# One attention layer, unrolled over the batch: maxima alone in the double PSUM banks, three single banks for everything that ScalarE empties

## The chip, the core and the metric

The kernel runs on one core of a Trainium2 chip. A core has five engines that run their own instruction streams and wait for each other by semaphores: TensorE (PE in the profile, with PEld for its weight loads), VectorE (DVE), ScalarE (ACT), GpSimd (POOL) and SyncE (SP, which here only issues transfers). TensorE writes to PSUM alone, a memory of eight banks of 2 KB per partition; VectorE and ScalarE read it. The metric is the time of the program in microseconds (us) of device time.

## The reference

A pre-norm transformer layer for x of shape [8, 1024, 256]:

- attention: LayerNorm; q, k, v = three 256x256 products (q and v with a bias); the last 256 of 1024 positions of q and k are rotated (cos, sin, in bf16); 16 heads of 16; softmax(q k^T / 4) v in float32; a 256x256 product with bias; added to x.
- mixture of experts: LayerNorm; gate logits (16 experts), softmax; each expert takes its 128 best tokens of a batch entry, runs a gated 256-512-256 network, and adds the result, weighted, to those tokens; a shared expert of the same shape runs on all tokens.

The change touches attention alone.

## The kernel before, in words

Attention handles one batch entry of 1024 tokens in a **turn** (`turn`, eight of them). Turn 0 and turn 7 stand in the code by themselves; turns 1 to 6 are one loop body (`Fori` in `turns`). Sixteen heads make four groups `g` of four heads; four heads lie at partitions 0, 32, 64 and 96, so four products with 32 rows each can run in the array side by side (`tile_position`).

A turn has 64 **steps**. A step takes one group, one half of the queries (512) and one tile of 128 keys. TensorE computes four blocks of transposed scores (`score_bank`, L858, keys on the partitions, 512 queries in a bank), ScalarE turns each into exp(score/4) in SBUF (L714, tile `PR`), and TensorE multiplies these with the values into one accumulator bank (`weigh_values`, L872, `pv`). Eight steps fill the accumulator for a query half; ScalarE copies it out (`evacuate`, L678, tile `OT`).

The softmax needs each query's maximum before the exponential. So the same scores are computed a second time in the other orientation (L800, queries on the partitions, two heads by 512 keys in a double bank), and VectorE reduces them (L554, tile `MX`), one group ahead. GpSimd splits the maximum in three bf16 parts (`split_maxima`), TensorE transposes them (L807), VectorE copies them to SBUF and four small transfers write them into spare rows of the transposed queries `QT`, where a -1 in `KT` subtracts them from the scores.

All other work is a list of **items** that `slot_items` puts among the steps: `xt` (transposed normalised input), `qk` and `v` (the projections; each product is made of three float32r products, L61 to L63), `qkT` (transposed q and k, L792), `ot` (transposed weighted values, L813), `aot` and `proj` (output projection), `x2t` and `lg` (gate logits, L842), and `sc` and `nm` (maxima scores and their parts).

The eight banks: two double banks `ring`, through which every item goes in turn; three single banks `st` for the transposed scores; one for `pv`. Within a step TensorE issues three `score_bank`, the first half of the step's items, the fourth `score_bank`, the value product of the step before, and then the other items. An item waits until the item two before it has been emptied, mostly by VectorE (`consume`); ScalarE empties only a few. At the end of turns 0 to 6 both `v` items are computed with nothing beside them (`flush`).

The lines that the prediction touches:

```python
                        for j in range(3):
                            score_bank(b, g, s, j)
                        for item in items[:cut]:
                            fill(item, t, b)
                        score_bank(b, g, s, 3)
                        if g or s:
                            finish_step(t, b, g * STEPS + s - 1)
```

Of the kernel before, what the change touches and what calls it, by code (L numbers as in the profile page):

```python
# [65 lines left out]
def attention(nc, d, ident, SC, B):  # L66
# [3 lines left out]

# [5 lines left out]
    NQ = T // 512  # L76
    STEPS = NQ * TT
    ROPE_TILES = 2
    SC_TILES = 4 * TT
    HALF = SC_TILES // NQ  # L80
    LEAD = 8
    ST_BANKS = 3
    P_STEPS = 2

    def scores(grp, a, z):

        return [("sc", grp, n % HALF // (TT // NQ), n // HALF * (TT // NQ) + n % (TT // NQ)) for n in range(a, z)]

    def last_score(grp, qh):
        return ("sc", grp, 3, TT // NQ * (qh + 1) - 1)

    def slot_items(g, prev, more):


        t = g + 1
        base = (scores(g, HALF + LEAD, SC_TILES) + scores(t, 0, 2) + [("nm", g, 1)] + scores(t, 2, HALF + 4)
                + [("nm", t, 0)] + scores(t, HALF + 4, HALF + LEAD))
        steps = [[] for _ in range(STEPS)]
        for n, item in enumerate(base):
            steps[n * STEPS // len(base)].append(item)
        extra = {3: [("ot", g - 1, 1)], 11: [("ot", g, 0)]}
        extras = [{2: [("qkT", 2)], 4: [("aot", 0, 1)], 5: [("aot", 1, 1)], 7: [("proj", 0)], 12: [("proj", 1)]},
                  {1: [("qkT", 3)], 2: [("xt", 0, 1)], 4: [("xt", 1, 1)], 9: [("qk", 0, 1)], 12: [("qk", 1, 1)], 14: [("qk", 2, 1)]},  # L110
                  {1: [("qk", 3, 1)], 6: [("x2t", 0)], 8: [("qkT", G)], 13: [("x2t", 1)]},
                  {1: [("qkT", G + 1)], 5: [("lg", 0)], 6: [("lg", 1)]}][g]
        for s, items in extras.items():
            extra[s] = extra.get(s, []) + items
        for s, items in extra.items():
            steps[s] = items + steps[s]

        def kept(i):
            if not more and (i[0] in ("xt", "qk") or (i[0] in ("sc", "nm", "qkT") and i[1] >= G)):
                return False  # L120
            return prev or not (i[0] in ("aot", "proj", "x2t", "lg") or i[:2] == ("ot", -1))
        return [[i for i in st if kept(i)] for st in steps]

    PRO = ([("xt", 0, 0), ("xt", 1, 0)] + [("qk", n, 0) for n in (3, 0, 1, 2)] + [("qkT", 0), ("qkT", 1), ("v", 0), ("v", 1)]
           + scores(0, 0, HALF + 4) + [("nm", 0, 0)] + scores(0, HALF + 4, HALF + LEAD))
    TAIL = [("ot", -1, 1), ("aot", 0, 0), ("aot", 1, 0), ("proj", 0), ("proj", 1), ("x2t", 0), ("x2t", 1), ("lg", 0), ("lg", 1)]

    def split_late(item):


        return item[0] in ("xt", "aot") and item[2] == 1

    def by_scalar(item):
        return split_late(item) or item[0] == "x2t"

    KINDS = {"all": lambda item: True, "vector": lambda item: not by_scalar(item), "scalar": by_scalar,
             "split": split_late}

    class Turn:

        def __init__(self, b, prev=False, more=False):
            self.kind = b if isinstance(b, str) else "turn"
            self.slots = [slot_items(g, prev, more) for g in range(G)] if self.kind == "turn" else []
            self.flush = [("v", 0), ("v", 1)] if more else []
            self.order = {"prologue": PRO, "tail": TAIL,
                          "turn": [i for sl in self.slots for st in sl for i in st] + self.flush}[self.kind]
            self.b, self.prev = b, prev

        def total(self, kind="all"):
            return len([i for i in self.order if KINDS[kind](i)])

        def before(self, kind="all"):
            if self.kind == "prologue":
                return 0
            n = Turn("prologue").total(kind)
            if self.kind == "tail":
                return n + Turn(0, False, True).total(kind) + (B - 2) * Turn(1, True, True).total(kind) + \
                    Turn(1, True, False).total(kind)  # L160
            if not self.prev:
                return n
            return n + Turn(0, False, True).total(kind) + (self.b - 1) * Turn(1, True, True).total(kind)

        def upto(self, item, kind="all"):

            return self.before(kind) + len([i for i in self.order[:self.order.index(item) + 1] if KINDS[kind](i)])

        def pair(self, item):

            first = self if self.kind != "turn" or not self.prev else Turn(1, True, True)
            return (first.before() + self.order.index(item)) % 2

        def vector_done(self, item):

            assert not by_scalar(item)
            return self.upto(item, "vector")

    assert Turn(1, True, True).total() % 2 == 0 and B > 1

    def turns(engine, body):

        body(0, False, True)
        if B > 2:
            with engine.Fori(1, B - 1) as b:
                body(b, True, True)
        body(B - 1, True, False)

    ctx = ExitStack()
    with ctx:  # L190
# [10 lines left out]
        b_q = sb("b_q", [P, H], F32)  # L201
        b_v = sb("b_v", [P, H], F32)
        b_o = sb("b_o", [P, H], F32)
        cs_in = sb("cs_in", [P, 2, ROPE_TILES, HD], F32)
# [4 lines left out]
        XN = sb("XN", [P, TT, H], F32)  # L209
# [6 lines left out]
        QP = sb("QP", [P, TT, NH, QUAD], BF16)  # L216
        KP = sb("KP", [P, TT, NH, QUAD], BF16)
        KT = [sb(f"KT{g}", [P, T], BF16) for g in range(G)]
        QT = [sb(f"QT{g}", [P, T], BF16) for g in range(G)]
        VA = sb("VA", [P, TT, NH, QUAD], F32)  # L220
        PR = [sb(f"PR{n}", [P, 4, 512], F32) for n in range(P_STEPS)]
        OT = sb("OT", [P, 512], F32)
        AO = sb("AO", [P, TT, H], F32)
        W_raw = AO[:].rearrange("p a c -> p (a c)").rearrange("p (k n) -> p k n", k=KH)
        NS = sb("NS", [12, T], BF16)
        MX = sb("MX", [P, 2, 2, 4, TT], F32)
        NM = sb("NM", [P, TT, 4, 3], BF16)
        nmr = sb("nmr", [P, 4, TT], F32)
        RD = sb("RD", [P, 2, 4, 4], F32)
        stats = sb("stats", [P, TT, 6], F32)  # L230

# [10 lines left out]
        act_scratch = sb("act_scratch", [P, 2], F32)  # L242
        dve_scratch = sb("dve_scratch", [P, 1], F32)
        pool_scratch = sb("pool_scratch", [P, 2], F32)

        ring = [ctx.enter_context(nc.psum_tensor(f"ring{i}", [P, 2, 512], F32)) for i in range(2)]
        st_bank = [ctx.enter_context(nc.psum_tensor(f"st{i}", [P, 512], F32)) for i in range(ST_BANKS)]
# [8 lines left out]
        xn2_ready = [sem(f"xn2_ready{h}") for h in range(2)]  # L256
# [3 lines left out]
        high_ready = sem("high_ready")  # L260
        split_ready = sem("split_ready")
        powers_ready = sem("powers_ready")
        const_ready = sem("const_ready")
        fills = sem("fills")
        bias_added = sem("bias_added")
        xn_ready = [sem(f"xn_ready{h}") for h in range(2)]
        rstd_ready = [sem(f"rstd_ready{n}") for n in range(2)]
        ring_full = sem("ring_full")
        vector_freed = sem("vector_freed")
        scalar_freed = sem("scalar_freed")  # L270
        rope_done = sem("rope_done")
        maxima_ready = sem("maxima_ready")
        nm_ready = sem("nm_ready")
        nm_in = sem("nm_in")
        st_full = sem("st_full")
        st_free = sem("st_free")
        pv_done = sem("pv_done")
        ot_ready = sem("ot_ready")
        dve_own = sem("dve_own")
        pool_own = sem("pool_own")  # L280

        N_CONST = 6
# [4 lines left out]
        def _(sp):  # L287
# [7 lines left out]
            sp.dma_start(b_q[:], d["bq"].partition_broadcast(P)).then_inc(const_in, 16)  # L295
            sp.dma_start(b_v[:], d["bv"].partition_broadcast(P)).then_inc(const_in, 16)
# [5 lines left out]
            def load_maxima(grp, qh, after):  # L302

                sp.wait_ge(vector_freed, after)
                c = slice(512 * qh, 512 * qh + 512)
                for j in range(4):
                    sp.dma_start(QT[grp % G][QUAD * j + HD:QUAD * j + HD + 3, c],
                                 NS[3 * j:3 * j + 3, c]).then_inc(nm_in, 16)

            pro = Turn("prologue")  # L310
            load_maxima(0, 0, pro.vector_done(("nm", 0, 0)))

            def store_x1(b):
                sp.dma_start(rows("out", b), XR[:]).then_inc(x1_out, 16)

            def store_xn2(b):
                for h in range(2):
                    sp.wait_ge(xn2_ready[h], b + 1)
                sp.dma_start(rows("xn2", b), XN2[:]).then_inc(xn2_out, 16)

            def turn(b, prev, more):
                t = Turn(b, prev, more)
                if more:
                    for h in range(2):
                        sp.wait_ge(xn_ready[h], b + 1)
                    sp.dma_start(XA[:], rows("x", b + 1)).then_inc(xa_in, 16)
# [1136 lines left out]
```

## Time and profile before

| what | us |
|---|---|
| time, median of 3 runs | 2822.38 (2801.42 to 2823.64) |
| the profiled execution's own time | 2783.07 |
| its span, first to last instruction | 2781.2 |
| attention, first to last value product | 75.7 to 1850.8 |
| experts | from about 1885 |

The profile has, for each instruction, its engine, its line in the code, its start and its duration. A timeline row merges neighbours of the same kind; the bracket at its end says how long the engine sat idle before it and which instruction released it. TensorE's clock has two levels, 1.2 and 2.4 GHz; the granted clock of a stretch is given as a share of the higher.

### The profile page before, as it was taken

The page shows a single profiled execution, that of the slowest core. Times are in us where ns is not written, and L with a number is a line of the kernel's source. Part 1 is how long each engine was busy: PE and PEld are TensorE (multiplying, and loading weights), DVE is VectorE, ACT ScalarE, POOL GpSimd, SP SyncE. Part 2 cuts the span into 40 slices and gives each one's busy share as a digit, 9 for nine tenths or more (in the row PEclk, how much of TensorE's full clock was granted, in tenths as well). Part 3 has the DMA queues.
Part 4 walks back from the last instruction along what each step waited for, and adds up shares of the span by engine and source line. Part 5 has one row for each costly group of instructions (what it writes and reads, how often), then busy time and mean ns, then how long its engine had stood idle before and what let it go on. Part 6 is the DMA issues. An engine that isn't in the chain of part 4 may idle for free. (4 is left out here: it accounts for less than half of the span.)

```text
span 2781.2 us, 47867 instructions
## 1 busy us (share of the span) xinstructions
PE 2437.5 (88%) x16011; PEld 1353.1 (49%) x16011; DVE 1985.0 (71%) x2856; ACT 1466.4 (53%) x2656; POOL 779.2 (28%) x1242
## 2 busy tenths in 40 slices
PE   5888888888888888888888888878999799999997
PEld 3232332333333333233333232237888688888886
DVE  7888888688788788778878879725666455555553
ACT  0667667567566566656756767733233233333331
POOL 1121231132122132122213211100000266666664
PEclk8799999899999989899989999958999899999998
DMA  1000000010000000001000000103222244444443
GB/s 38 16 17 16 17 32 2 18 33 16 18 17 32 18 17 32 5 30 32 2 18 17 32 2 17 32 27 117 90 90 83 84 101 106 104 105 104 105 106 40
DMA packets 105805, 124.20 MB, mean 45 GB/s; under 512 B 8049, under 2 KB 92785, under 8 KB 105585
## 3 DMA queue, kind: packets, MB, share of 16 engines
q1 hardware_dynamic: 81008, 87.81, 9.9%
q0 software_dynamic: 24576, 33.57, 7.1%
q8 instruction: 124, 2.03, 0.3%
q14 instruction: 97, 0.79, 0.1%
HBM read 78.63 MB, written 41.94 MB: 43 GB/s over the span
## 5 line engine op out<-in xcount | busy, mean ns | idle before, releaser
L714 ACT ACTIVATE sb_PR<-st 128x512 f32<-128x512 f32 x2048 | 1092.0, 602 | 679.8 <-PE st L858 674.0
L554 DVE TENSOR_REDUCE sb_MX<-ring 128x2 f32<-128x1024 f32 x1024 | 1211.3, 1219 | 140.5 <-PE ring L800 111.6
L872 PE MATMUL pv<-sb_PR,sb_VA 128*32 128x512 f32 x4096 | 589.2, 650 | 1.2
L858 PE MATMUL st<-sb_QT,sb_KT 32*128 32x512 bf16 x2048 | 502.9, 405 | 81.7 <-ACT sb_PR L714 69.4
L800 PE MATMUL ring<-sb_KT,sb_QT 32*128 32x512 bf16 x2048 | 422.8, 406 | 151.0 <-DVE sb_MX L554 139.6
L359 POOL TENSOR_TENSOR sb_pool_scratch<-identity 128x1 f32<-128x1 f32 x284 | 55.2, 194 | 1346.1 <-DVE sb_MX L586 1327.4
L800 PEld LDWEIGHTS ring<-sb_KT,sb_QT 32*128 32x128 bf16 x2048 | 98.3, 92 | 679.9 <-DVE sb_MX L554 445.3
L1235 DVE TENSOR_TENSOR ex_HF<-ex_GL,ex_gu 128x512 f32<-128x512 f32 x128 | 87.5, 684 | 251.7 <-ACT ex_GL L1168 238.9
L1168 ACT ACTIVATE ex_GL<-ex_gu 128x512 f32<-128x512 f32 x128 | 76.5, 598 | 348.2 <-PE ex_gu L63 243.1
L858 PEld LDWEIGHTS st<-sb_QT,sb_KT 32*128 32x128 bf16 x2048 | 130.4, 92 | 225.1 <-ACT sb_PR L714 184.2
L1132 POOL DMA_INDIRECT out<-ex_YS,ex_rows_out x128 | 209.0, 1633 | 44.1 <-issue 43.6
L61 PE MATMUL ex_gu<-ex_XH,weights_high 128*128 128x512 f32 x512 | 200.8, 392 | 2.4 <-DVE ex_XL L1227 2.4
L62 PE MATMUL ex_gu<-ex_XL,weights_high 128*128 128x512 f32 x512 | 200.5, 392 | 0.0
L63 PE MATMUL ex_gu<-ex_XH,weights_low 128*128 128x512 f32 x512 | 200.2, 391 | 0.0
L1089 POOL TENSOR_TENSOR ex_pool_scratch<-identity 128x1 f32<-128x1 f32 x96 | 35.2, 366 | 526.7 <-POOLq L932 380.7
L872 PEld LDWEIGHTS pv<-sb_PR,sb_VA 128*32 128x32 f32 x4096 | 82.8, 111 | 160.0 <-issue 92.2
L61 PE MATMUL ex_y<-weights_high,ex_HH 128*128 128x256 f32 x512 | 148.1, 289 | 2.9 <-DVE ex_HL L1239 2.9
L62 PE MATMUL ex_y<-weights_low,ex_HH 128*128 128x256 f32 x512 | 145.5, 284 | 0.0
L63 PE MATMUL ex_y<-weights_high,ex_HL 128*128 128x256 f32 x512 | 145.5, 284 | 0.0
L1110 POOL DMA_INDIRECT ex_XG<-xn,ex_rows_in x128 | 126.1, 985 | 40.2 <-issue 39.6
L1168 ACT ACTIVATE sh_GL<-sh_gu 128x512 f32<-128x512 f32 x64 | 38.2, 597 | 177.0 <-PE sh_gu L63 177.0
L1235 DVE TENSOR_TENSOR sh_HF<-sh_GL,sh_gu 128x512 f32<-128x512 f32 x64 | 43.7, 683 | 104.4 <-ACT sh_GL L1168 104.2
(160 smaller groups left out, 3946.7 us busy)
## 6 DMA issues: line engine op xcount, KB each, us to landing
sb_XA<-x SPq DMA_DIRECT2D x8, 1024.0 KB, 5.6
sb_XR<-x SPq DMA_DIRECT2D x8, 1024.0 KB, 5.3
out<-sb_XR SPq DMA_DIRECT2D x8, 1024.0 KB, 4.5
xn<-sb_XN SPq DMA_DIRECT2D x8, 1024.0 KB, 4.5
sh_XG<-xn SPq DMA_DIRECT2D x16, 512.0 KB, 5.6
sh_X<-out SPq DMA_DIRECT2D x16, 512.0 KB, 5.0
weights<-WgT SPq DMA_DIRECT2D x16, 512.0 KB, 4.2
weights<-WuT SPq DMA_DIRECT2D x16, 512.0 KB, 6.2
```

The source lines that it names most:

```text
L61: nc.tensor.matmul(out, a_hi, b_hi, start=first, stop=False)
L62: nc.tensor.matmul(out, a_hi, b_lo, start=False, stop=False)
L63: return nc.tensor.matmul(out, a_lo, b_hi, start=False, stop=last)
L554: out = nc.vector.reduce_max(MX[:, grp % 2, half, 2 * pair:2 * pair + 2, qt], R[:], AX.X)
L714: nc.scalar.activation(PR[step % P_STEPS][:, j, :], st_bank[n % ST_BANKS][:], ACT.Exp, scale=0.25).then_inc(st_free, 1)
L800: out = nc.tensor.matmul(R[:, n, :], QT[grp % G][r, P * qt:P * qt + P], KT[grp % G][r, 512 * half:512 * half + 512], start=True, stop=True ...
L858: nc.tensor.matmul(st_bank[n % ST_BANKS][:], KT[g][r, P * kt:P * kt + P], QT[g][r, 512 * qh:512 * qh + 512], start=True, stop=True, tile_p ...
L872: out = nc.tensor.matmul(pv_bank[QUAD * j:QUAD * j + QUAD, :], VA[:, kt, 4 * g + j, :], PR[step % P_STEPS][:, j, :], start=(kt == 0), stop ...
L1110: nc.gpsimd.indirect_dma_start(out=XG[k % 2][:, t, :], out_offset=None, in_=d["xn2"], in_offset=bass.IndirectOffsetOnAxis(ap=rows_in[:, b: ...
L1132: nc.gpsimd.indirect_dma_start(out=d["out"], out_offset=bass.IndirectOffsetOnAxis(ap=rows_out[:, b:b + 1], axis=0), in_=YS[k % 2][:, t, :] ...
L1168: nc.scalar.activation(GL[f % 2][:], gu[f % 2][:, 0, 0:N], ACT.Gelu).then_inc(gelu_ready, 1)
L1235: nc.vector.tensor_tensor(HF[f % 2][:], GL[f % 2][:], gu[f % 2][:, 1, 0:N], ALU.mult).then_inc(hf_ready, 1)
```

## The change

Attention is written anew; the experts are as before.

- No loop: all 8 x 64 = 512 steps `V` stand in the code one after the other.
- The double banks `ring` hold only scores for maxima (`score_rows`, two per step, 12 steps ahead, `LEAD`). VectorE does these reductions, and its statistics, but no longer empties other items.
- The three single banks are now called `rot`. The transposed scores (`score_turned`) and every other item pass through them in one order (`ORDER`), and ScalarE empties all of them (`empty`). Items are cut to the size of one bank, so there are more, smaller ones; at most one stands in a step (`BESIDE`).
- Within a step TensorE issues maxima scores, transposed scores 0 and 1, maxima scores, transposed scores 2 and 3, then the item, then the value product of two steps before (`LAG`).
- The maxima's parts are written by GpSimd into spare columns of `QP`, and q is transposed once more for each half group (item `q2`); the small transfers are gone.
- The bias of q is added on TensorE by two products with one row; that of v is folded into the output bias once. `v` items stand in steps 49 to 58 and `VA` and `QP` exist twice. The projection's result goes by ScalarE to `PJ`, and GpSimd adds it to the residual.

```diff
-    ST_BANKS = 3
-    P_STEPS = 2
+    LEAD, LAG = 12, 2
+    ROT = 3
+    P_STEPS = 3
+    BESIDE = {
+        0: ("aot", -1, 0, 0), 1: ("aot", -1, 1, 0), 2: ("qT", 0, 2, 0), 3: ("ot", 7), 4: ("qT", 0, 2, 1),
+        5: ("proj", -1, 0), 6: ("q2", 1), 7: ("aot", -1, 0, 1), 8: ("aot", -1, 1, 1), 9: ("proj", -1, 1),
+        11: ("ot", 0), 12: ("proj", -1, 2), 14: ("q2", 2), 15: ("proj", -1, 3), 16: ("qT", 0, 3, 0), 17: ("qT", 0, 3, 1),
+        19: ("ot", 1), 20: ("xt", 1, 0, 0), 21: ("xt", 1, 1, 0), 22: ("q2", 3), 23: ("xt", 1, 0, 1), 24: ("xt", 1, 1, 1),
+        26: ("qk", 1, 6), 27: ("ot", 2), 28: ("qk", 1, 7), 30: ("q2", 4), 31: ("qk", 1, 0), 33: ("qk", 1, 1),
...
-        body(0, False, True)
-        if B > 2:
-            with engine.Fori(1, B - 1) as b:
-                body(b, True, True)
-        body(B - 1, True, False)
...
+            def bank(item):
+
+                n = PLACE[item]
+                if n >= ROT:
+                    pe.wait_ge(rot_done, n - ROT + 1)
+                return rot[n % ROT]
...
+            for V in range(-LEAD, LAST):
+                m = 2 * (V + LEAD)
+                if m < CHECKS:
+                    score_rows(m)
+                if V >= 0:
+                    for j in range(2):
+                        score_turned(V, j)
+                if m < CHECKS:
+                    score_rows(m + 1)
+                if V >= 0:
+                    for j in range(2, 4):
+                        score_turned(V, j)
+                for item in beside(V):
+                    fill(item)
+                if V >= LAG:
+                    weigh_values(V - LAG)
...
+            for V in range(-LEAD, LAST):
+                if V >= 0:
+                    for j in range(4):
+                        empty(("ex", V, j))
+                        if j == 2 and V >= 9 and V % 8 == 1:
+                            evacuate((V - 9) // 8)
+                for item in beside(V):
+                    empty(item)
```

How it moves instructions on TensorE, at a step with an `ot` item in turn 0. Before (`ring` L800 is for maxima, `st` L858 the transposed scores, L813 the item, L872 the values):

```order
L872 MATMUL pv<-sb_PR,sb_VA 32x512 x4
L800 MATMUL ring<-sb_KT,sb_QT 128x512 x2
L858 MATMUL st<-sb_QT,sb_KT 128x512 x3
L813 MATMUL ring<-identity,sb_OT 128x128 x4
L800 MATMUL ring<-sb_KT,sb_QT 128x512 x2
L858 MATMUL st<-sb_QT,sb_KT 128x512
L872 MATMUL pv<-sb_PR,sb_VA 32x512 x4
```

Now (L773 is for maxima, `rot` L786 the transposed scores, L740 the item, L797 the values):

```order
L797 MATMUL pv<-sb_PR,sb_VA 32x512 x4
L773 MATMUL ring<-sb_KT,sb_QT 128x512 x2
L786 MATMUL rot<-sb_QT,sb_KT 128x512 x2
L773 MATMUL ring<-sb_KT,sb_QT 128x512 x2
L786 MATMUL rot<-sb_QT,sb_KT 128x512 x2
L740 MATMUL rot<-identity,sb_OT 128x128 x4
L797 MATMUL pv<-sb_PR,sb_VA 32x512 x4
```

The item has moved from ahead of the fourth transposed score to behind it, and from a double bank to the rotation of three.

On ScalarE, around the copy of the accumulator. Before, in turn 0, it stood between the first and the second exponential of a step (in the loop body, where each instruction has a row):

```order
L714 ACTIVATE sb_PR<-st 128x512
L720 ISA
L678 COPY sb_OT<-pv 128x512
L713 REGISTER_ALU
L714 ACTIVATE sb_PR<-st 128x512
```

Now it stands between the third and the fourth, and the other items (L600, L604 and L605, L623) follow the fourth:

```order
L591 ACTIVATE sb_PR<-rot 128x512 x4
L600 COPY sb_XT<-rot 128x512
L591 ACTIVATE sb_PR<-rot 128x512 x3
L641 COPY sb_OT<-pv 128x512
L591 ACTIVATE sb_PR<-rot 128x512 x5
L604 CAST sb_QP<-rot 128x16x16
L605 CAST sb_KP<-rot 128x16x16
```

The copy waits for the value product that the same step issues last.

## Rows read from the trace of the kernel before

**Rows 1.** The page: TensorE's granted clock in 40 equal slices, in tenths.
```profile
PEclk8799999899999989899989999958999899999998
```

**Rows 2.** Groups by line: count, busy us, mean ns, idle us before them, releaser.
```profile
L714 ACT ACTIVATE sb_PR<-st 128x512 f32<-128x512 f32 x2048 | 1092.0, 602 | 679.8 <-PE st L858 674.0
L554 DVE TENSOR_REDUCE sb_MX<-ring 128x2 f32<-128x1024 f32 x1024 | 1211.3, 1219 | 140.5 <-PE ring L800 111.6
L678 ACT COPY sb_OT<-pv 128x512 f32<-128x512 f32 x64 | 37.1, 580 | 2.5 <-PE pv L872 2.5
L414 POOL TENSOR_TENSOR sb_AL<-sb_XT,sb_AH 128x1024 fp32r<-128x1024 f32 x14 | 33.1, 2364 | 1.1
```

**Rows 3.** Windows: length, PE, PEld, DVE, ACT, POOL busy us, clock, DMA share, GB/s.
```profile
494.00:1640.00 1146.00, 984.47 (x6950) 376.99 (x6946) 928.56 (x1292) 725.28 (x1359) 277.99 (x545) 0.93 0.06 20
```

**Rows 4.** Timeline (start, length, engine, line): first scores of turns 0, 1, 7.
```profile
71.19 0.61 PE L858 MATMUL st<-sb_QT,sb_KT 32*128 32x512 bf16 x3 [0.44 <-DMA sb_QT<-sb_NS]
...
282.39 0.39 PE L858 MATMUL st<-sb_QT,sb_KT 32*128 32x512 bf16 x3
...
1638.10 0.39 PE L858 MATMUL st<-sb_QT,sb_KT 32*128 32x512 bf16 x3
```

**Rows 5.** Timeline, a step without other items, turn 0.
```profile
118.12 0.45 PE L858 MATMUL st<-sb_QT,sb_KT 32*128 32x512 bf16 x3
118.67 2.06 ACT L714 ACTIVATE sb_PR<-st 128x512 f32<-128x512 f32 x4 [0.60 <-PE st L858]
119.32 0.38 PE L858 MATMUL st<-sb_QT,sb_KT 32*128 32x512 bf16 x1 [0.44 <-ACT sb_PR L714]
119.63 1.07 PE L872 MATMUL pv<-sb_PR,sb_VA 128*32 128x512 f32 x8
```

**Rows 6.** Timeline, another such step, turn 7.
```profile
1789.84 1.07 PE L872 MATMUL pv<-sb_PR,sb_VA 128*32 128x512 f32 x8
1790.84 0.86 PE L858 MATMUL st<-sb_QT,sb_KT 32*128 32x512 bf16 x3
1792.32 1.07 PE L872 MATMUL pv<-sb_PR,sb_VA 128*32 128x512 f32 x8
```

**Rows 7.** Timeline, a step with an `ot` item, turn 1.
```profile
681.10 1.07 PE L872 MATMUL pv<-sb_PR,sb_VA 128*32 128x512 f32 x8
...
682.82 0.66 PE L813 MATMUL ring<-identity,sb_OT 128*128 128x128 f32 x4
...
684.49 1.06 PE L872 MATMUL pv<-sb_PR,sb_VA 128*32 128x512 f32 x8
```

**Rows 8.** Timeline, TensorE at the end of turn 1: `v` items, loop, next turn.
```profile
495.39 0.39 PE L61 MATMUL ring<-sb_WH,sb_XH 128*128 128x256 f32 x1
...
501.13 0.28 PE L63 MATMUL ring<-sb_WH,sb_XL 128*128 128x256 f32 x1
503.18 0.61 PE L858 MATMUL st<-sb_QT,sb_KT 32*128 32x512 bf16 x3 [1.77 <-issue]
...
508.18 0.60 PE L800 MATMUL ring<-sb_KT,sb_QT 32*128 32x512 bf16 x2 [3.55 <-DVE sb_MX L554]
```

**Rows 9.** Timeline, other items on TensorE: `qk`, `qkT`, `lg`.
```profile
608.61 0.50 PE L61 MATMUL ring<-sb_WH,sb_XH 128*128 128x512 f32 x1
...
611.24 0.39 PE L63 MATMUL ring<-sb_WH,sb_XL 128*128 128x512 f32 x1
...
569.86 0.62 PE L792 MATMUL ring<-sb_identb,sb_QP 128*128 128x128 bf16 x8
...
688.98 1.96 PE L842 MATMUL ring<-sb_gw,sb_XT 128*128 128x16 f32 x16
```

**Rows 10.** Timeline, turn 7 when no maxima are left: value products, low clock.
```profile
1840.72 1.94 PE L872 MATMUL pv<-sb_PR,sb_VA 128*32 128x512 f32 x8
...
1844.48 1.94 PE L872 MATMUL pv<-sb_PR,sb_VA 128*32 128x512 f32 x8
```

**Rows 11.** Timeline, ScalarE ahead of TensorE, turn 1.
```profile
703.20 3.69 ACT L714 ACTIVATE sb_PR<-st 128x512 f32<-128x512 f32 x7
```

More of the change, by code:

```diff
@@ L75, in attention @@
     KH = H // P
-    NQ = T // 512
-    STEPS = NQ * TT
+    STEPS = G * 2 * TT
+    UNITS = 2 * G
+    LEAD, LAG = 12, 2
     ROPE_TILES = 2
-    SC_TILES = 4 * TT
-    HALF = SC_TILES // NQ
-    LEAD = 8
-    ST_BANKS = 3
-    P_STEPS = 2
[L92 to L177, printed above, removed]
@@ new lines, in attention @@
+    HEAD = ([("xt", 0, h, half) for half in range(2) for h in range(KH)] + [("qk", 0, i) for i in (6, 7, 0, 1, 2, 3, 4, 5)]
+            + [("qT", 0, 0, 0), ("qT", 0, 0, 1), ("bo",)])
+    TAIL = ([("ot", UNITS * B - 1)] + [("aot", B - 1, h, half) for half in range(2) for h in range(KH)]
+            + [("proj", B - 1, i) for i in range(4)] + [("x2t", B - 1, h, half) for half in range(2) for h in range(KH)]
+            + [("lg", B - 1, half) for half in range(2)])
+    ORDER = HEAD + [item for V in range(-LEAD, LAST)
+                    for item in ([("ex", V, j) for j in range(4)] if V >= 0 else []) + beside(V)] + TAIL
@@ L189, in attention, with done, check @@
+    PLACE = {item: n for n, item in enumerate(ORDER)}
+    assert len(PLACE) == len(ORDER)
+    def done(item):
+        return PLACE[item] + 1
+    def check(m):
+        unit, n = m // 16, m % 16
+        c = (2, 0, 3, 1)[n % 4]
+        return unit, c // 2, c % 2, 4 * (unit % 2) + n // 4
     ctx = ExitStack()
@@ L497, in normalise @@
-            def normalise(n, out, src, ready, own):
-                for k in range(RSQRT_STEPS):
-                    own.inc(rstd_step(n, k, own))
-                own.wait(dve)
+                step = rsqrt_step(nc, k, rstd[n][:], nt1[:], nt2[:], mv[n][:, :, 1])
+                if k == RSQRT_STEPS - 1:
+                    step.then_inc(rstd_ready[n], 1)
+                else:
+                    own.inc(step)
+            def normalise(n, b, out, src, ready):
+                dve.wait_ge(rstd_ready[n], b)
@@ L648, in _ @@
-            turns(dve, turn)
-            own = Tally(dve_own, HEAD + PER_FIRST + (B - 2) * PER + PER - LN_INCS)
-            tail = Turn("tail")
-            for item in TAIL[:3]:
-                consume(item, tail, B, own)
-            for half in range(2):
-                consume(("proj", half), tail, B, own)
-                x1_stands(tail.vector_done(("proj", half)), own)
-                statistics(1, XR, range(TT // 2 * half, TT // 2 * (half + 1)), own)
-            own.wait(dve)
-            dve.wait_ge(xn2_out, 16 * (B - 1))
@@ L742, in _ @@
[L742 removed]
+                empty(item)
+            gate_powers(B - 1)
         @block.tensor
@@ L902, in _ @@
+            for V in range(LAST - LAG, LAST):
+                weigh_values(V)
             for item in TAIL:
-                fill(item, Turn("tail"), B)
+                fill(item)
 KD, KF = D // P, F // P
```

896 lines of the change are left out of this document (434 added, 462 removed), and 5 rows, old and new, of the table BESIDE.

## The prediction

> **What bounds the kernel now.** I read the page first, then the groups by line, then the timeline of TensorE and ScalarE step by step. The groups show two engines with large reductions: ScalarE's exponentials are busy 1092 us and wait 674 us for the transposed scores; VectorE's maxima are busy 1211 us and wait little [rows 2]. In the middle turns VectorE is busy 929 of 1146 us, TensorE 984, ScalarE 725 [rows 3]. No engine is full, so the time is set by a chain that goes round between engines, and the question is how long it is in a step.
>
> A step with nothing beside it shows the chain. Three transposed scores start at 118.12; ScalarE starts at 118.67; the fourth score needs the bank of the first and starts at 119.32, which is 1.20 after the first; the values start at 119.63, 0.31 later [rows 5]. From the value product to the next step's scores it is 1.00 [rows 6]. Together 1.00 + 1.20 + 0.31 = 2.51 us; rows 6 show 2.48 from one value product to the next. Four exponentials take 2.06 in a row [rows 5], two maxima about 2.4 [rows 2]: both fit under it. **The bound is this loop through three single banks**, to which items add.
>
> A turn takes (1638.10 - 282.39) / 6 = 226.0 us in the middle, turn 0 takes 211.2 [rows 4], turn 7 takes 213 (the attention's end is in the table).
>
> **What goes.** At the end of turn 1 TensorE computes `v` alone (495.39 to 501.3), sits 1.77 us with nothing to wait for, and then 3.55 us for VectorE [rows 8]. All of it goes. The Trainium skill (Runtime: NRT & Kernel Launch, "Instruction fetch mechanics") says that a taken branch breaks the sequential prefetch; the 1.77 us agree, and by that rule alone the change should gain. Also VectorE's waits for items, and TensorE's for VectorE, go; I count them in by building the new turn from steps rather than by subtracting. The transfers of the maxima go too; they are hidden behind a lead of several steps before, and their successor `q2` stands two steps ahead of its use and three behind the last maximum, some 9 us for five GpSimd operations on 16 elements: nothing for that.
>
> **What comes: the item now lies on the chain.** Before, the first half of a step's items stood in the 1.20 us in which TensorE waits for the first exponential anyway. An `ot` item made a step of 3.39 us [rows 7], part of it a wait for VectorE. Now the item comes behind the fourth score and takes the bank after it in the rotation, so it waits for the second exponential: four take 2.06 [rows 5], so one comes every 0.52 us. The item starts 0.52 behind the fourth score, and then its own length f, and then the values. So a step with an item takes 1.00 + 1.20 + 0.52 + f = 2.72 + f; one without, 2.5.
>
> The lengths f at the high clock:
> - four float32 transposes: 0.66 with the drain of the last [rows 7], about 0.50 to the next instruction; 12 (`xt`, `aot`, `x2t`) and 8 `ot`: 10.0 us
> - eight bf16 transposes 0.62 with the drain [rows 9], about 0.45; 8 `qT` 3.6, and 8 `q2` of four at 0.3 2.4
> - `qk`: eleven intervals in 2.63 us [rows 9], six products and their lead 1.5, two short bias products 0.25 (estimate, from the 0.12 below): 8 x 1.75 = 14.0
> - `v` and `proj`: 47 intervals in 5.74 us, 0.122 each [rows 8]; twelve products 1.5; 8 x 1.5 = 12.0
> - `lg`: 1.96 [rows 9], 1.9 to the next; 2 x 1.9 = 3.8
>
> Sum 45.8. `BESIDE` has 54 items: 10 x 2.5 + 54 x 2.72 + 45.8 = 217.7 us.
>
> **The accumulator's copy.** Once in eight steps ScalarE copies `pv` between the third and fourth exponential, and waits for the value product that TensorE issues last in that step, behind the item. Counted from the fourth score: item from 0.52 to 1.02, values to 2.09 (their length is 1.07 [rows 5]), copy from about 2.2, fourth exponential 2.7, item's copy 3.2, next exponential 3.7. Without the copy the next exponential would start at 1.02 + 1.00 + 0.5 = 2.5. So 1.2 us each, 0.7 in the one step without an item, 1.6 with a long copy: 9.6 us per turn. Bounds: nothing if ScalarE had slack (in the kernel before such copies wait 2.5 us in all [rows 2]), 12 if the copy's 0.58 [rows 2] does not overlap its neighbours. I take 9.6, since the order leaves no other.
>
> **GpSimd** must split two `aot` parts between the maxima of step 3 and `proj` of step 5; the second operation of each split takes 2.4 us on 1024 elements [rows 2], 1.2 on 512, and with the first ones and the five small operations ahead about 5 us go by, where the order leaves 4 to 5: I take 0.8 us per turn, bounds 0 and 2. Its other work lies more than a step ahead of need, and so do the residual's store and load before `add_bias`.
>
> Middle turn: 217.7 + 9.6 + 0.8 = 228.1 at the high clock. Before, the clock was 0.93 in the middle turns [rows 3], that is 14% of the time at 1.2 GHz. There a step takes 3.76 us [rows 10], half as much again. Some of that followed the idle end of the turn, which goes. I take 3 us per turn for what is left (bounds 0 and 14% x 1/3 x 228 = 11): 231, against 226.0. Six turns: +30.
>
> Turn 0: 39 items, f 31.5, seven copies 8.5: 62.5 + 106.1 + 40.0 = 208.6, and the low clock at its start as before (the third slice [rows 1] lies there; about 27 us, a third of them lost, 9): 218 against 211, +7. Turn 7: 33 items, f 21.7: 77.5 + 89.8 + 21.7 + 9.6 = 198.6, and the last 12 steps have no maxima beside them, in which the clock was low before: 12 x 1.25 = 15; 214 against 213. Start and end: finer items, same engines; I take nothing, bounds 5 us each way.
>
> **Sum**: 30 + 7 + 0 = +37 us. The profiled execution took 2783.07, so 2820; the median of the runs shown is 2822.38, 1.4% above it, and the difference carries over: **2860 us**.
>
> **Rivals.**
> 1. *The clock falls as often as before, or more.* For: every item's step leaves TensorE waiting twice (1.20 less the maxima scores, and 0.52), and the steps after the copy wait 1.2 more. Against: turns 0 and 7 run long stretches of 2.5 to 3.4 us steps with the clock full. Price: 11 us per turn in place of 3, some 45 us: 2905. The Trainium skill (TensorE: Matmul & The Clock Gate, "A second HAM failure mode: psum-queue depth-cycling") tells of a clock that goes up and down when TensorE idles briefly between groups while cycling through PSUM banks; by that rule this rival would be the forecast.
> 2. *Faster: ScalarE works ahead.* In some stretches ScalarE is never idle: seven exponentials in 3.69 us [rows 11]. Where it has a bank of work in hand when TensorE comes back from the values, the loop's latency is hidden, the step is set by ScalarE's and VectorE's busy time, and the item's 0.52 us wait is nothing. For: VectorE, which held items up, is relieved. Against: with an item the rotation has only two banks for scores, less in hand than before. It decides from one item in five: 54 x 0.52 x 8 = 225 us in all, so a fifth pays for the 37. Price at a bit over half of that plus nothing else, 0.57 x 225 = 128: 2732; at 0.4, 90: 2770, which I take.
> 3. *No change.* The copy stall is half hidden (-38) and the clock stays full (-18): 2804.
>
> **Numbers.** Forecast 0.42; rival 1 0.15; rival 2 0.20; rival 3 0.23. About 1% can be told from no change. Faster by over 1% (below 2794): most of rival 2, a bit of the others, 0.25. Within: most of rival 3 and the lower part of the forecast, 0.31. Slower (above 2851): 0.44. Each step's 0.1 us is 51 us over 512 steps, so the forecast alone reaches from 2815 to 2905; with rival 3 below, part of rival 2 and rival 1, the range is 2755 to 2925, leaving out the far end of rival 2 and a clock worse than before.
>
> **What would show it.** In the new timeline: value product to value product 2.5 us without and 3.2 us with a short item; the item 0.52 behind the fourth score, released by an exponential; ScalarE's copy from `pv` waiting about 1.2 us for TensorE; VectorE's maxima waiting for scores, TensorE hardly for VectorE; no gap at a turn's end; a middle turn of 231 us. It would be wrong if steps with items took under 3.0 us, if the copy's wait did not move the next exponential, or if the granted clock in the middle differed much from 0.97.

## The result, and the profile after

| | before | changed |
|---|---|---|
| median of the runs, us | 2811.9 (2797.12 to 2823.64, 4 runs) | 2926.68 (2897.88 to 2933.39, 4 runs) |
| ratio | | 1.0391, 95% interval 1.0298 to 1.0485 |
| the profiled execution, us | 2783.07 | 2933.39 |
| its granted clock, mean of the span | 0.937 | 0.903 |

The changed kernel is slower, as forecast, but by 3.9% where 2860 against 2822.38 meant 1.3%. The median lies 1.7 us above the upper end of the range. Ratios, here and below, leave out runs over 1.5% above the fastest of the same kernel; medians and ranges count all.

The two profiled executions lie further apart than the medians, 150 us against 115: the one of the kernel before is faster than its four timed runs, and the one of the changed kernel is the slowest of its four, at the lowest clock (0.903; the others 0.908 to 0.922).

The page of the changed kernel, TensorE's clock in 40 slices (before: [rows 1]):

```profile
PEclk8898989799789878988999897896999999999998
```

In attention, the first 28 slices, 7 and 8 stand in place of many 9s. The groups by line (count, busy, mean ns, idle before them, releaser), of the page and, for L641, of the view by lines; before: [rows 2]:

```profile
L450 DVE TENSOR_REDUCE sb_MX<-ring 128x2 f32<-128x1024 f32 x1024 | 1218.4, 1221 | 598.0 <-PE ring L773 595.1
L591 ACT ACTIVATE sb_PR<-rot 128x512 f32<-128x512 f32 x2048 | 1068.3, 606 | 369.1 <-PE rot L786 367.4
L786 PE MATMUL rot<-sb_QT,sb_KT 32*128 32x512 bf16 x2048 | 600.1, 428 | 231.4 <-ACT sb_PR L591 221.8
L641 ACT COPY sb_OT<-pv 128x512 f32<-128x512 f32 x64 | 37.5, 585 | 125.5 <-PE pv L797 125.5
```

VectorE now waits 598 us for scores, and the time that TensorE's maxima scores wait for VectorE fell from 139.6 to 49.9 us. What is left has two long waits in each of turns 1 to 6: 1.27 to 1.55 us in step 14 and 1.88 in step 30. And a new wait stands in the last line: 125.5 us in 64 copies of the accumulator, where it was 2.5. Windows over the five turns 2 to 6, the middle turns in what follows (from one `gate_powers`, which comes once a turn, to the fifth after it: length, busy time of PE, PEld, DVE, ACT, POOL, granted clock), the changed kernel:

```profile
543.71:1786.52 1242.81, 1046.44 (x6964) 358.80 (x6960) 843.24 (x1076) 830.78 (x1636) 283.61 (x390) 0.87 0.05 17
```

and the kernel before, five turns as well, from its own marks, which stand seven steps earlier:

```profile
471.21:1607.96 1136.75, 976.07 (x6884) 370.70 (x6880) 923.98 (x1286) 723.68 (x1356) 277.99 (x545) 0.93 0.06 20
```

That is 248.6 us per turn against 227.4. Cut at the first transposed scores of turn 2 (544.85, before 503.18) and of turn 7 (1787.66, before 1638.10) and at the last value product, the difference of the profiled executions, 150 us, lies thus: start and turns 0 and 1 +42, turns 2 to 6 +108, turn 7 +6, what follows -5. The slow part is the middle.

A step without an item, the changed kernel's timeline (start, length, what ended the idle time before it), TensorE:

```profile
120.06 1.06 PE L797 MATMUL pv<-sb_PR,sb_VA 128*32 128x512 f32 x8
...
121.68 0.88 PE L786 MATMUL rot<-sb_QT,sb_KT 32*128 32x512 bf16 x2
122.49 1.06 PE L797 MATMUL pv<-sb_PR,sb_VA 128*32 128x512 f32 x8
```

and one with an `ot` item:

```profile
708.53 1.06 PE L797 MATMUL pv<-sb_PR,sb_VA 128*32 128x512 f32 x8
...
710.64 0.38 PE L786 MATMUL rot<-sb_QT,sb_KT 32*128 32x512 bf16 x1 [0.50 <-ACT sb_PR L591]
711.13 0.66 PE L740 MATMUL rot<-identity,sb_OT 128*128 128x128 f32 x4
711.71 1.07 PE L797 MATMUL pv<-sb_PR,sb_VA 128*32 128x512 f32 x8
```

2.43 and 3.18 us, where 2.5 and 3.22 were forecast; the item starts 0.49 behind the fourth score, forecast 0.52. The timeline around a copy of the accumulator, TensorE:

```profile
831.64 1.06 PE L797 MATMUL pv<-sb_PR,sb_VA 128*32 128x512 f32 x8
832.64 0.39 PE L773 MATMUL ring<-sb_KT,sb_QT 32*128 32x512 bf16 x2
832.64 0.38 PE L786 MATMUL rot<-sb_QT,sb_KT 32*128 32x512 bf16 x1
833.91 0.39 PE L786 MATMUL rot<-sb_QT,sb_KT 32*128 32x512 bf16 x1 [0.89 <-ACT sb_PR L591]
...
835.21 1.06 PE L797 MATMUL pv<-sb_PR,sb_VA 128*32 128x512 f32 x8
```

and ScalarE in the same stretch:

```profile
828.89 1.57 ACT L591 ACTIVATE sb_PR<-rot 128x512 f32<-128x512 f32 x3 [0.64 <-PE rot L786]
832.77 0.58 ACT L641 COPY sb_OT<-pv 128x512 f32<-128x512 f32 x1 [2.31 <-PE pv L797]
833.25 0.60 ACT L591 ACTIVATE sb_PR<-rot 128x512 f32<-128x512 f32 x1
833.74 0.59 ACT L630 COPY sb_PJ<-rot 128x512 f32<-128x512 f32 x1
```

ScalarE has done three exponentials by 830.5 and stands still until the values of 831.64 are in. The fourth exponential, whose scores have lain in their bank since about 829.9, and the item's copy queue behind it. So the next step's second score finds no bank for 0.89 us, and this step, without an item, takes 3.57 us, 1.14 more than 2.43. This is the **stall** of what follows: a transposed score that waits 0.8 us or more for an exponential. What the forecast did not have comes next. Another such place:

```profile
735.24 0.39 PE L786 MATMUL rot<-sb_QT,sb_KT 32*128 32x512 bf16 x1 [0.88 <-ACT sb_PR L591]
...
737.29 1.66 PE L797 MATMUL pv<-sb_PR,sb_VA 128*32 128x512 f32 x8
...
740.75 1.11 PE L740 MATMUL rot<-identity,sb_OT 128*128 128x128 f32 x4
```

The eight value products take 1.66 us and not 1.06: the clock has fallen to 1.2 GHz during them, and the transposes after them take 1.11 for 0.66. Counting value products of over 1.2 us that follow one of 1.06: in the changed kernel the clock fell 50 times within attention, before 18 times. 43 steps have a stall, always the step behind a copy; 34 of the 50 falls came in such a step or in the one after it. The other 16 recur at two places of a turn: 12 in or just behind a step with an `lg` item, and 4 in steps 30 and 31, with or after the 1.88 us wait for VectorE, which in the other two turns no fall follows.

From the timeline of every step the five middle turns can be added up. Each of 319 intervals from one value product to the next is set against the median of its kind of item at the high clock in the changed kernel. A stalled step counts in the row of the stalls alone, whatever its clock:

| us in five middle turns | changed | copy moved (experiment 1) | filler (experiment 4) |
|---|---|---|---|
| all steps at their medians | 1078.3 | 1078.3 | 1078.3 |
| more in steps with a value product of over 1.1 us at either end | 111.3 (92 steps) | 68.7 (56) | 53.1 (42) |
| more in stalled steps | 39.2 (30 stalls) | 0 | 41.6 (30) |
| other | 9.2 | 15.5 | 15.3 |

### The profile page after: what moved, and what is told of

Its sections match the earlier page's. It is cut to its first block and busy times, and to the rows that moved or that the text cites. A ratio compares the mean times of both kernels' runs of the same rounds, so it can differ in the third digit from the quotient of the medians.

```text
span 2931.6 us, 41961 instructions
## 1 busy us (share of the span) xinstructions
PE 2536.6 (87%) x16142; PEld 1342.3 (46%) x16142; DVE 1861.4 (63%) x2545; ACT 1640.8 (56%) x3104; POOL 784.6 (27%) x987
## 5 line engine op out<-in xcount | busy, mean ns | idle before, releaser
L591 ACT ACTIVATE sb_PR<-rot 128x512 f32<-128x512 f32 x2048 | 1068.3, 606 | 369.1 <-PE rot L786 367.4
L786 PE MATMUL rot<-sb_QT,sb_KT 32*128 32x512 bf16 x2048 | 600.1, 428 | 231.4 <-ACT sb_PR L591 221.8
L797 PE MATMUL pv<-sb_PR,sb_VA 128*32 128x512 f32 x4096 | 636.4, 698 | 0.0
L773 PE MATMUL ring<-sb_KT,sb_QT 32*128 32x512 bf16 x2048 | 394.7, 429 | 52.3 <-DVE sb_MX L450 49.9
L786 PEld LDWEIGHTS rot<-sb_QT,sb_KT 32*128 32x128 bf16 x2048 | 124.8, 93 | 525.8 <-ACT sb_PR L591 490.1
L773 PEld LDWEIGHTS ring<-sb_KT,sb_QT 32*128 32x128 bf16 x2048 | 76.0, 94 | 591.5 <-DVE sb_MX L450 325.0
L310 POOL CAST sb_QP<-sb_MX 128x16 bf16<-128x16 f32 x64 | 16.2, 253 | 1208.6 <-DVE sb_MX L456 1208.6
L797 PEld LDWEIGHTS pv<-sb_PR,sb_VA 128*32 128x32 f32 x4096 | 85.1, 114 | 94.2 <-ACT sb_PR L591 36.9
L61 PE MATMUL rot<-sb_WH,sb_XH 128*128 128x512 f32 (+1 forms) x256 | 106.3, 415 | 13.1 <-DVE sb_XL L444 5.5
```

What stands on the lines that cost most here:

```text
L61: nc.tensor.matmul(out, a_hi, b_hi, start=first, stop=False)
L591: out = nc.scalar.activation(PR[V % P_STEPS][:, j, :], R[:], ACT.Exp, scale=0.25)
L773: out = nc.tensor.matmul(ring[m % 2][:, n, :], QT[g][r, P * qt:P * qt + P], KT[g][r, 512 * half:512 * half + 512], start=True, stop=True, ...
L786: nc.tensor.matmul(R[:], KT[g][r, P * kt:P * kt + P], QT[g][r, 512 * qh:512 * qh + 512], start=True, stop=True, tile_position=(r.start, 0) ...
L797: out = nc.tensor.matmul(pv_bank[head(j), :], VA[b % 2][:, kt, 4 * g + j, :], PR[V % P_STEPS][:, j, :], start=(kt == 0), stop=(kt == TT - 1))
```

## The experiments

Theory A, formed from this: the middle turns are long because the copy, standing behind the third exponential, waits for a product that TensorE issues last, and because the stalled TensorE then loses its clock. Against it stand the item's own wait on the chain (which the forecast had counted in full) and the clock falling for another reason. "Before" was timed anew beside each group: 2816.67, 2816.91 and 2810.77 us.

**1. The copy alone is moved** to the next step, behind its first exponential, when the values have long been written.

```diff
-                        if j == 2 and V >= 9 and V % 8 == 1:
-                            evacuate((V - 9) // 8)
+                        if j == 0 and V >= 10 and V % 8 == 2:
+                            evacuate((V - 10) // 8)
```

> The changed kernel with one edit: ScalarE's copy of the accumulator stands one step later, behind the first exponential, when the value product it waits for has long been issued. Theory A (the copy's stall costs time by itself and also makes TensorE's clock fall): the stall of 0.9 to 1.2 us goes 63 times, less some 0.4 us that the copy adds in its new place, so 50 us directly, and the granted clock in the middle turns rises from about 0.88 to 0.95 or more, worth another 60 to 100 us: 2770 to 2820. Theory B (the clock falls because every step with an item leaves TensorE waiting, wherever the copy stands): only the direct part, 2865 to 2885, clock still near 0.88.

Measured: **2813.94 us** (2802.12 to 2821.91, 10 runs), 1.0008 times before [0.9974 to 1.0041]: 113 us less than the changed kernel, and not to be told from the kernel before. The view by lines and the window over the same five turns:

```profile
L641 ACT COPY sb_OT<-pv 128x512 f32<-128x512 f32 x64 | 37.1, 580 | 4.3 <-PE pv L797 4.3
```
```profile
515.03:1680.49 1165.46, 968.94 (x6960) 344.14 (x6960) 840.45 (x1076) 829.82 (x1636) 283.55 (x390) 0.93 0.06 18
```

The wait is gone, a middle turn takes 233.1 us, the clock fell 20 times. The steps themselves are the same (medians 2.43 without an item, 3.19 with a short one), but for those that now hold the copy, which take 0.16 us more without an item and 0.49 with one. By the table above the five turns lost 39 us of stalls and 43 of low clock, of 77 in all: more than half of the gain is the clock's.

**2. The values ahead of the item**: `weigh_values` is called before the item's `fill`, the copy stays.

```diff
+                if V >= LAG:
+                    weigh_values(V - LAG)
                 for item in beside(V):
                     fill(item)
-                if V >= LAG:
-                    weigh_values(V - LAG)
```

> The changed kernel with one edit: within a step TensorE issues the value product ahead of the item instead of behind it. The item no longer adds its wait for the second exponential (0.52 less 0.31 us) to a step with an item: 0.2 us for 407 items, 80 us, and the copy of the accumulator waits some 0.5 us less, 25 us. Steps with a short item should take 2.95 us in place of 3.18. Theory A (copy's stall brings the clock down): the stall is only halved, clock rises a little, in all 2760 to 2830. Theory B (item's wait brings the clock down): the clock rises clearly, to 0.95, 2720 to 2770. If the item's wait is not on the chain: no more than 30 us, 2895 or above.

Measured: **2774.07 us** (2762.54 to 2778.3), 0.9864 [0.9785 to 0.9944]. The copy's wait is 38.3 us in all, a middle turn 224.0, the clock 0.97. A step with a short item of four transposes is 3.01 to 3.15 and not 3.19: the values lie in the item's wait for its bank. No stall is left of the 43, and the clock fell 13 times. The run does not decide between the expectation's two theories: its time lies in theory A's range, its clock is the one of theory B.

**3. Both edits.**

> Both edits of the two runs beside it: copy of the accumulator one step later, value product ahead of the item. If the two costs are separate their direct gains add: 50 + 80 = 130 us, and the clock is full save at start and end, 60 to 110 us more: 2690 to 2740, below the kernel before (2812). If the gains are one and the same slack: no better than the better of the two.

Measured: **2758.11 us** (2735.84 to 2761.8), 0.9802 [0.971 to 0.9894]; a middle turn 223.7, with the same steps as in 2. The clock fell 11 times. The expectation for gains that add, 2690 to 2740, is missed: they do not add, and both edits together are 16 us better than the second alone. Whichever edit starts the values or the copy at a time at which nobody waits takes the stall away, and there is one stall.

**4. The stall stays, and TensorE is given filler** just behind it: in the step after the copy the second pair of maxima products is issued six times (the same result is written again), which computes nothing new.

```diff
-                for n in range(2):
+                V = m // 2 - LEAD
+                for n in [0, 1] * (6 if m % 2 and V >= 10 and V % 8 == 2 else 1):
```

> The changed kernel, its order untouched; in the step after each copy of the accumulator TensorE issues the second pair of maxima scores six times over in place of once (same operands, same bank, same result), about 1.1 us of array work inside a wait of 2 us and more. The copy's stall stays. Theory A: the clock no longer falls behind the copy, so 60 to 110 us are won with the stall in place: 2815 to 2865, granted clock 0.95. Theory B: the clock falls elsewhere as often: 2915 to 2935. If the extra products delay the chain they add up to 0.3 us each, 20 us.

Measured: **2862.32 us** (2851.57 to 2872.95), 1.0199 [1.0111 to 1.0287]: 64 us less than the changed kernel, with more work. The timeline at a copy:

```profile
709.15 0.38 PE L787 MATMUL rot<-sb_QT,sb_KT 32*128 32x512 bf16 x1 [0.88 <-ACT sb_PR L591]
709.16 1.03 PE L774 MATMUL ring<-sb_KT,sb_QT 32*128 32x512 bf16 x7
...
711.35 1.07 PE L798 MATMUL pv<-sb_PR,sb_VA 128*32 128x512 f32 x8
```

The stall is there with its 0.88 us (the copies wait 121.8 us in all), and the values behind it run in 1.07. The clock fell 19 times, 3 of them in or just after a stall, though there are 43 stalls as before the edit. The window over five turns:

```profile
527.36:1718.88 1191.52, 995.77 (x7364) 361.26 (x7360) 843.15 (x1076) 831.30 (x1636) 283.94 (x390) 0.95 0.06 18
```

So the falls are a cost of their own, 64 us in the median of the runs and 58 in the table's five turns, and they can be taken away with the stall left in place.

**5. The mirror: the kernel before with its copy late**, between the third and fourth exponential, where the values it needs are issued last in the step.

```diff
-                            if j == 0 and s % TT == 1 and (prev or step > 1):
+                            if j == 2 and s % TT == 0 and (prev or step > 1):
```

> The kernel before with one edit: ScalarE's copy of the accumulator moves from behind the first exponential of the second step to between the third and fourth of the first step of a query half, so that it waits for the value product that this very step issues, as it does in the changed kernel. Theory A (a stalled copy costs its stall and the clock): 56 of 64 copies stall, 0.7 to 1.2 us each, 40 to 65 us, and the granted clock falls from 0.93 to about 0.90 in the middle, 30 to 60 us more: 2880 to 2940. Theory B (place of the copy does not matter for the clock): 2855 to 2880. If the stall hides in waits for VectorE in this kernel: under 2840.

Measured: **2919.23 us** (2906.85 to 2955.78), 1.0352 [1.0243 to 1.0461], clock 0.895 in the span. This one edit makes the kernel before as slow as the changed one. The clock fell 28 times and not 18, 11 of them in or just after one of 36 stalls; 18 of the 28 come at the first value product of a query half, right behind the late copy, where the kernel before has 7 of its 18. Its copies wait:

```profile
L678 ACT COPY sb_OT<-pv 128x512 f32<-128x512 f32 x64 | 37.7, 588 | 85.8 <-PE pv L872 85.8
```

**6. The item between the second and third transposed score**, on TensorE, in `ORDER` and on ScalarE, with the copy moved too. It was meant to use the time in which TensorE waits for the first exponential. The edit on TensorE:

```diff
+                for item in beside(V):
+                    fill(item)
                 if m < CHECKS:
                     score_rows(m + 1)
                 if V >= 0:
                     for j in range(2, 4):
                         score_turned(V, j)
-                for item in beside(V):
-                    fill(item)
```

> The changed kernel with the copy of the accumulator moved as in the first run, and each item put between the transposed scores 1 and 2, on TensorE, in the rotation and on ScalarE; the values stay last. If the item costs its place behind the fourth score, as predicted, its length is now hidden in the 1.20 us wait for the first exponential, and the rotation makes the fourth score wait for the second exponential instead: 3.0 us for a short item (3.18 now), 3.3 for a qk item (4.62) and 3.1 for a v item (4.21). A middle turn some 30 us shorter than with the copy moved alone (233): 200 to 210; 2560 to 2640. If TensorE or VectorE is the bound by then: not under 2700.

Measured: **2654.78 us** (2646.13 to 2661.4), 0.9404 [0.9334 to 0.9474]; a middle turn 208.8, the clock 0.97. It beats both kernels, but misses the 2560 to 2640 of its expectation. `qk` takes 3.56 us and `v` 3.48, where they took 4.62 and 4.21; 3.3 and 3.1 were expected. Of the steps without an item some take the 2.43 they took, others 2.6. No stall is left, and the clock fell 17 times.

**7. The same, with the copy left in its late place**, to part the two.

> The changed kernel with the item between the second and the third transposed score (on TensorE, in the rotation and on ScalarE), but with ScalarE's copy of the accumulator left between the third and fourth exponential, waiting for the value product that TensorE issues last. With copy moved as well this kernel took 2654.8. Theory A (the copy's stall, and the low clock that follows it, cost some 14 to 18 us per turn wherever the items stand, since the copy still waits for a product issued last in its step; only the item's own part of the wait is gone): copies still wait 0.4 to 0.9 us, the granted clock in the middle falls from 0.97 to about 0.90, 2720 to 2770. Rival B (the stall hurts only because the item and its bank wait stand ahead of the values; with the item served earlier the values start 1 us earlier and the copy finds them nearly done): copy wait under 0.3 us, clock 0.96 or more, 2650 to 2680.

Measured: **2658.05 us** (2653.31 to 2676.27), 0.944 [0.9342 to 0.9537]: the same time as 6. Theory A is wrong as worded here, and the rival in this expectation holds: the place of the copy does not decide. The view by lines:

```profile
L642 ACT COPY sb_OT<-pv 128x512 f32<-128x512 f32 x64 | 37.7, 589 | 22.4 <-PE pv L799 21.6
```

The copies wait 22.4 us in all and not 125.5, since the values follow the fourth score at once; no stall is left, and the clock fell 16 times. The timeline shows a step with an `aot` item:

```profile
713.24 1.06 PE L799 MATMUL pv<-sb_PR,sb_VA 128*32 128x512 f32 x8
714.23 0.39 PE L775 MATMUL ring<-sb_KT,sb_QT 32*128 32x512 bf16 x2
714.24 0.39 PE L788 MATMUL rot<-sb_QT,sb_KT 32*128 32x512 bf16 x2
714.47 0.38 PE L775 MATMUL ring<-sb_KT,sb_QT 32*128 32x512 bf16 x2
714.78 0.66 PE L682 MATMUL rot<-identity,sb_AO 128*128 128x128 f32 x4
715.36 0.86 PE L788 MATMUL rot<-sb_QT,sb_KT 32*128 32x512 bf16 x2
716.15 1.06 PE L799 MATMUL pv<-sb_PR,sb_VA 128*32 128x512 f32 x8
```

No row has a bracket: TensorE goes from product to product, and this step is set by TensorE alone. In the five middle turns:

```profile
478.25:1532.45 1054.20, 971.03 (x6964) 356.38 (x6960) 846.97 (x1076) 830.02 (x1636) 284.28 (x390) 0.97 0.06 20
```

TensorE is busy 971 of 1054 us, where it was busy 1046 of 1243. The idle time before the transposed scores fell from 231.4 to 57.1 us over attention.

**8. Only the values in that wait**, between the two middle transposed scores; the item stays last, the copy stays.

```diff
                 if m < CHECKS:
                     score_rows(m + 1)
+                if V >= LAG:
+                    weigh_values(V - LAG)
                 if V >= 0:
...
                 for item in beside(V):
                     fill(item)
-                if V >= LAG:
-                    weigh_values(V - LAG)
```

> The changed kernel with only the values put between the maxima scores and the transposed scores 2; items stay last, and the copy keeps its place. Steps without an item become 2.4 us by VectorE; with a short item the 1.00 us of the values leave the chain: 2.6 in place of 3.18, qk 3.6, v 3.2. A middle turn of 180 to 195 us, 2440 to 2560. With the run beside it this tells how much the item's place still matters once the values are off the chain: by the chain theory little for short items, some 0.4 us for each long one, 50 us in all.

Measured: **2686.89 us** (2684.43 to 2690.05), 0.9525 [0.9456 to 0.9594]. Faster than both kernels, but a miss against an expectation of 2440 to 2560: that took the chain as the only bound. A step with a short item takes 3.09 us with no idle time on TensorE in it either, and TensorE is busy 997 of 1057 us in the middle turns. It ran into the engine's own work.

**9. Values and item both in that wait**, in this order; `ORDER` and ScalarE as in 6, the copy stays. The edit on TensorE:

```diff
                 if m < CHECKS:
                     score_rows(m + 1)
+                if V >= LAG:
+                    weigh_values(V - LAG)
+                for item in beside(V):
+                    fill(item)
                 if V >= 0:
                     for j in range(2, 4):
                         score_turned(V, j)
-                for item in beside(V):
-                    fill(item)
-                if V >= LAG:
-                    weigh_values(V - LAG)
```

> The changed kernel with values and item, in this order, between the transposed scores 1 and 2 (item there also in the rotation and on ScalarE); the copy of the accumulator keeps its place. Values and item then stand in the wait for the first exponential, and the chain of 2.43 us is cut: what is left is ScalarE's own work, 0.52 us for each exponential and copy, 2.6 us for a step with an item, VectorE's 2.4, and TensorE's 1.0 + f + 0.6. A middle turn of 175 to 190 us: 2420 to 2520. If the chain was not the bound: 2700 or more.

Measured: **2888.0 us** (2882.36 to 2895.05), 1.0249 [1.0173 to 1.0326], a clear miss. TensorE with a `qk` item:

```profile
662.05 1.06 PE L799 MATMUL pv<-sb_PR,sb_VA 128*32 128x512 f32 x8
...
665.88 0.89 PE L788 MATMUL rot<-sb_QT,sb_KT 32*128 32x512 bf16 x2 [0.62 <-ACT sb_KP L606]
...
666.91 1.06 PE L799 MATMUL pv<-sb_PR,sb_VA 128*32 128x512 f32 x8
```

and ScalarE:

```profile
660.87 2.06 ACT L592 ACTIVATE sb_PR<-rot 128x512 f32<-128x512 f32 x4
665.18 0.37 ACT L605 CAST sb_QP<-rot 128x256 bf16<-128x256 f32 x1 [2.24 <-PE rot L711]
665.45 0.38 ACT L606 CAST sb_KP<-rot 128x256 bf16<-128x256 f32 x1
```

ScalarE empties in the order of the rotation, so it waits 2.24 us for an item that stands behind 1.06 us of values, with exponentials queued behind it, and their banks are what TensorE wants next. The step takes 4.86 us where it took 3.56 in experiment 6. The wait of TensorE was filled with its own work, and ScalarE's was made longer.

## Why the prediction was right in sign and short in size

- **What bounds the kernel before**: a loop of three single banks, 2.5 us in a step. It holds: 2.43 in the changed kernel and with its copy or item elsewhere (experiments 1 and 6).
- **The item on the chain, 2.72 + f**: it holds for each kind. Medians at the high clock against the forecast: short transposes 3.19 (3.22), `q2` 2.93 (3.02), `qT` 3.15 (3.17), `v` and `proj` 4.21 (4.22), `qk` 4.62 (4.47), `lg` 4.49 (4.62). At its medians a middle turn makes 1078.3 / 5 = 215.7 us, and 1 more with the one interval that the table leaves out; forecast 217.7.
- **The accumulator's copy, 1.2 us each, 9.6 per turn**: the mechanism was foreseen. A stalled step took 1.14 to 1.71 us more, in part at the low clock; six of a turn's eight copies had a stall, 39.2 / 5 = 7.8 us per turn. The forecast gave 0.7 to a copy with no item ahead of its values; the runs show no stall there, nor in experiments 2 and 7, where no item stands between the fourth score and the values.
- **The clock, 3 us per turn: this is the term that was mis-sized.** It took 111.3 / 5 = 22.3 us. A middle turn was forecast at 231.1 and took 248.6. The difference of 17.5 is the clock's 19.3 more, less 1.0 of the steps and 1.8 of the stalls, and 9.2 / 5 = 1.8 of other waits against 0.8 for GpSimd. Over six turns it is 105 us, against 113 by which the profiled execution missed 2820. The forecast counted on the idle end of the turn going and the clock getting better for it. The window of before says 0.93 and the changed kernel's 0.87, where the prediction named a clock that differed much from 0.97 as a sign of being wrong. How much the clock loses varies from run to run: the changed kernel's four runs lie between 2897.88 us at 0.922 and 2933.39 at 0.903, and the profiled one, from which the 22.3 is taken, is the slowest. Rival 1 had this mechanism and its place ("the steps after the copy wait 1.2 more"), with a chance of 0.15 and 11 us per turn, a price that its bound held down. That bound was the fault: it took the share of time at the low clock of the kernel before as the most there could be, while most falls come with the stalls (34 of 50), and the change brought 43 of these.
- By the Trainium skill (TensorE: Matmul & The Clock Gate, "A second HAM failure mode: psum-queue depth-cycling") short idle times between groups in a cycle of banks make the clock go up and down. Experiment 1 keeps that cycle and all its waits of 0.4 to 0.5 us and has 20 falls, against 18 in the kernel before; only the waits of 0.88 on top brought the others. The rule named the right danger, and experiment 1 the wait that brought it here.
- **What went**: no gap is left at a turn's end and VectorE's items are off the chain, as forecast. The forecast had TensorE hardly wait for VectorE; 49.9 us of such waits are left. **Start**: forecast 0 within 5 us, measured +7 (the first transposed scores at 78.53, before 71.19 [rows 4]); TensorE's `v` items now stand between the first maxima scores. No run tested it. **End**: forecast 0, measured -5.
- **Rival 2**, faster because ScalarE works ahead, did not come: it decides where ScalarE has a bank in hand, and with the item last it rarely has: in 73 of 512 steps none of its four exponentials waits, and 367.4 us of its idle time are waits for transposed scores. With the item in the middle there are 138 and 151 such steps (experiments 6 and 7), and the sign is the one this rival had.

Of the 272 us between the changed kernel and experiment 6, the copy's place accounts for 113 when moved alone and for 3 (not to be told from nothing) when the item has been moved. Why the other 16 of the 50 falls came where they did stays open. Experiment 1 has its 20 at such places too: 11 in or just behind a step with `lg`, 5 in step 30 and 4 in step 14. No run was made to take those away.

## What to carry to other kernels

Where two engines hand banks to each other in a fixed order, put the work that needs no hand-over at the place where an engine waits anyway, and look in the same step at what the other engine will be waiting for: experiments 7 and 9 differ only in the place of the values, and by 230 us. A copy of an accumulator belongs where its last product is long written; behind a product that is issued last in a step, after other work, it stops the queue behind it. And a stall's price is its length and the clock after it; here the clock's part was the larger: experiment 4 took away 64 us of clock, where experiment 1 took away clock and stall for 113.

## What the runs showed of the hardware

- A wait of TensorE of 0.88 us on top of waits of 0.5 us in the steps around it was followed by the lower clock, in the same step or the next, in 34 of 43 cases. With ten more short products with 32 rows right behind the stall (TensorE busy from 709.16 on where it had waited) that was so in 3 of 43, and all falls went from 50 to 19. A longer wait, 1.88 us for VectorE in step 30, had a fall with or after it in 4 of 6 turns, and one of 1.27 to 1.55 us in step 14 in none of 6: length alone does not tell.
- The filler was cheap, and not free: the step with it took 4.47 us (706.88 to 711.35), the one of the changed kernel at its twin 4.40 (704.13 to 708.53); step 10 of a turn took 3.88 for 3.57, and step 18 the same 3.99.
- 512 steps as straight code cost TensorE no time that shows: its shortest step took 2.43 us, as did the shortest full steps of the loop body, and the idle 1.40 to 1.87 us before each of turns 2 to 6 ([rows 8] has the first, 1.77) were gone.
